# Strided TENSOR_REDUCE for pair minimum and maximum, a list meeting through PSUM, and a reordered pipeline on SyncE, GpSimd, ScalarE and TensorE

## The reference

```python
dist = jnp.sqrt((diff * diff * m_h).sum(axis=-1) + 1e-08)   # to the 64 tokens of the causal window
dist = jnp.where(mask[None], dist, jnp.inf)
neg_d, loc = jax.lax.top_k(-dist, K)                        # K = 32 nearest of 64
infl = jnp.exp(-topd); infl = infl / (infl.sum(-1, keepdims=True) + 1e-08)
context = jnp.einsum('btk,btkd->btd', infl, neighbor_v)
context = context + gate * 0.1 * (q_unit @ (hebb_U[h] @ hebb_V[h]))
outs.append(q_h * context)                                  # then the decoder, the second norm and the experts
```

## Time and profile before

| quantity | value |
|---|---|
| median of three runs | 994.27 us |
| profiled execution, time / span | 990.1 / 988.3 us |
| busy: TensorE, VectorE, ScalarE, GpSimd | 748.7, 771.6, 501.0, 521.6 us |
| mean granted TensorE clock | 0.722 of full speed |
| first and last theta reduction (64 of them) | 98.7 and 958.0 us |

### The profile page before, as it was taken

The page is one execution under the profiler, slowest core; times in us unless marked ns, Lnnn a source line. Parts: engine busy times, 40 slices in busy tenths (PEclk is TensorE's granted clock), DMA queues, the critical chain, the costliest instruction groups (busy, mean ns, idle before and its releaser), DMA issues. The chain is left out here.

```text
span 988.3 us, 21942 instructions
## 1 busy us (share of the span) xinstructions
PE 748.7 (76%) x5686; PEld 534.6 (54%) x5749; DVE 771.6 (78%) x5082; ACT 501.0 (51%) x1542; POOL 521.6 (53%) x811
## 2 busy tenths in 40 slices
PE   5977776777687766678688767789688777788765
PEld 3444554554465545555466546566466554666554
DVE  5857998788778887778787787788887887787861
ACT  3952455554455445544455445554455544555452
POOL 2113475555645565556655565565655656555452
PEclk8985777887857688876766686765766777766665
DMA  5300000000000000000000000000000000000000
GB/s 158 97 3 13 14 10 18 16 17 15 19 18 15 14 19 19 16 15 16 19 18 15 14 19 18 15 17 16 18 19 15 18 14 19 19 16 17 15 14 11
DMA packets 41181, 21.18 MB, mean 21 GB/s; under 512 B 6040, under 2 KB 40544, under 8 KB 41056
## 3 DMA queue, kind: packets, MB, share of 16 engines
q1 hardware_dynamic: 41056, 19.77, 7.0%
HBM read 10.44 MB, written 4.19 MB: 15 GB/s over the span
## 5 line engine op out<-in xcount | busy, mean ns | idle before, releaser
L984 DVE MAX8 gsgn_all<-modn_all 128x8 f32<-128x32 f32 x2048 | 204.2, 172 | 0.0
L740 ACT ACTIVATE nst<-psC 16x192 f32<-16x192 f32 x64 | 20.5, 320 | 287.6 <-PE psC L1276 287.6
L990 DVE MATCH_REPLACE8 modn_all<-gsgn_all,modn_all 128x32 f32<-128x32 f32 x1024 | 166.1, 173 | 0.0
L554 POOL TENSOR_TENSOR big<-big,con 128x512 f32<-128x512 f32 x128 | 162.7, 1293 | 4.8 <-DVE big L1033 4.8
L505 POOL TENSOR_SCALAR n_c<-x,nm_c,rs_c 128x128 f32<-128x128 f32 x64 | 29.4, 460 | 248.4 <-ACT nm_c L678 244.5
L1235 PE MATMUL psC<-vst,big 128*128 128x68 f32 x512 | 120.6, 324 | 43.1 <-ACT n L781 41.5
L1015 DVE SCALAR_TENSOR_TENSOR key<-psD,key 128x512 f32<-128x512 f32 x64 | 44.1, 690 | 126.5 <-ACT key L701 126.3
L1193 PE MATMUL psD<-mask_bf,ident_bf 128*128 128x320 bf16 x256 | 69.9, 419 | 94.3 <-DMA tst<-nst 93.3
L1235 PEld LDWEIGHTS psC<-vst,big 128*128 128x128 f32 x512 | 97.8, 238 | 54.5 <-issue 51.2
L1236 PE MATMUL psC<-vst,big 128*128 128x68 f32 x512 | 120.8, 325 | 0.0
L1236 PEld LDWEIGHTS psC<-vst,big 128*128 128x128 f32 x512 | 99.0, 240 | 0.0
(11 more groups left out here) (208 smaller groups left out, 1795.0 us busy)
## 6 DMA issues: line engine op xcount, KB each, us to landing
tst<-qT_all SPq DMA_DIRECT2D x256, 17.0 KB
big<-in_x SPq DMA_DIRECT2D x16, 256.0 KB, 2.9
xs<-in_x SPq DMA_DIRECT2D x64, 64.0 KB, 1.9
out<-yo SPq DMA_DIRECT2D x64, 64.0 KB, 1.6
sst<-nst SPq DMA_DIRECT2D x128, 3.0 KB
tst<-nst SPq DMA_DIRECT2D x128, 2.0 KB
con<-in_consts SPq DMA_DIRECT2D x1, 581.5 KB, 6.1
wmod_sb<-in_wmod SPq DMA_DIRECT2D x1, 384.0 KB, 4.5
```

What stands on the lines that cost most here:

```text
L554: nc.gpsimd.tensor_tensor(wab[:, k % 2, v].rearrange("p (r t) -> p r t", r=4), wsel.rearrange("p (r t) -> p r t", r=4), part.unsqueeze(1). ...
L984: last = v.max(top[:, u, h, where], low_high[:, u, h])
L990: last = v.match_replace(low_high[:, u, h], top[:, u, h, 0:8], low_high[:, u, h], GONE)
```

## The change

- VectorE: the maximum, the minimum and the negation become two TENSOR_REDUCE instructions over a view whose innermost dimension is the pair, 32 elements apart. `meet` no longer reads two lists from SBUF: the negated high list is written to PSUM (`pHigh`, in bank 1 of `psW`) and `meet` reads it there. Den and reciprocal of chunk i-2 move ahead of `d2` and of `drop(1)`.
- SyncE: the output DMA goes to the end of the step, behind the rows.
- GpSimd: `sqs` and `sst` go ahead of `n_c`.
- PSUM: `pN` and `pNN` move from `psC` into free columns of bank 0 of `psW`.
- TensorE: context products first, then the `diff` transposes, values, `pN` (i+3), `pNN` (now i+2), counting and the rest. The context products no longer wait for `n2`; the key transposes now wait for `nst` of chunk i+3 and `n2` of chunk i+2.
- ScalarE: `lnn`/`rnn` go to the front, `cst` ahead of the Signs, `vst`, `nst` and `n2` (now i+2) behind the Signs, the last Exp to the end of the step.

The PSUM columns:

```diff
+        pHigh = psW[:, 1, 0:2 * NH * 8].rearrange("p (h n) -> p h n", h=NH)
         pC = psC[:, 0:8 * VP]
-        pN = psC[0:2 * NH, 8 * VP:8 * VP + 3 * WIN]
-        pNN = psC[:, 8 * VP + 3 * WIN:8 * VP + 3 * WIN + NH]
+        pN = psW[0:2 * NH, 0, 3 * WIN:6 * WIN]
+        pNN = psW[:, 0, 6 * WIN:6 * WIN + NH]
```

SyncE:

```diff
             def step(i):
-                k = i - 4
-                if there(k):
-                    sync.wait_ge(yo_ready, k + 1)
-                    sync.dma_start(oc[:, k], yo[:, k % 2]).then_inc(out_in[k % 2], 16)
                 k = i + 3
...
                     sync.dma_start(xs[:, k % 4], xc[:, k]).then_inc(xs_in[k % 4], 16)
+                k = i - 4
+                if there(k):
+                    sync.wait_ge(yo_ready, k + 1)
+                    sync.dma_start(oc[:, k], yo[:, k % 2]).then_inc(out_in[k % 2], 16)
```

VectorE, pairs and meeting:

```diff
-                    x4 = key[:, i % 2].rearrange("p (h u j) -> p h u j", h=NH, u=2)
+                    x4 = key[:, i % 2].rearrange("p (h u j) -> p h j u", h=NH, u=2)
                     dve.wait_ge(d2_ready, i + 1)
                     need(dve, theta_ready, i)
-                    v.tensor_tensor(low_high[:, 1], x4[:, :, 0], x4[:, :, 1], ALU.max).then_inc(pair_done, 1)
-                    v.tensor_tensor(low_high[:, 0], x4[:, :, 0], x4[:, :, 1], ALU.min).then_inc(pair_done, 1)
-                    dve.wait_ge(pair_done, 3 * i + 1)
-                    v.tensor_scalar(low_high[:, 1], low_high[:, 1], -1.0, None, ALU.mult).then_inc(pair_done, 1)
-                    dve.wait_ge(pair_done, 3 * i + 2)
+                    v.tensor_reduce(low_high[:, 0], x4, AX_X, ALU.min).then_inc(pair_done, 1)
+                    v.tensor_reduce(low_high[:, 1], x4, AX_X, ALU.max, negate=True).then_inc(pair_done, 1)
+                    dve.wait_ge(pair_done, 2 * i + 1)
...
-                    v.scalar_tensor_tensor(out=meet, in0=top[:, 1], scalar=-1.0, in1=top[:, 0], op0=ALU.mult,
+                    need(dve, w_ready, i)
+                    v.tensor_scalar(pHigh, top[:, 1], -1.0, None, ALU.mult).then_inc(high_done, 1)
+                    dve.wait_ge(high_done, i + 1)
+                    v.scalar_tensor_tensor(out=meet, in0=pHigh, scalar=0.0, in1=top[:, 0], op0=ALU.max,
                                            op1=ALU.max).then_inc(meet_done, 1)
```

TensorE, the products ahead of counting, and the waits ahead of the key transposes:

```diff
+                k = i + 3
+                if there(k):
+                    need(pe, n2_ready, k - 1)
+                    pe.wait_ge(opnd_ready, k + 1)
+                    for g in range(NG):
+                        last = mm(pN, selm[:, k // CPB, g], sqs[:, g], start=(g == 0), stop=(g == NG - 1))
+                    last.then_inc(pn_ready, 1)
+                k = i + 2
+                if there(k):
+                    pe.wait_ge(nst_ready, k + 1)
+                    mm(pNN, nst[:, k % 2, WIN:3 * WIN], con[0:2 * NH, C_ID + NH:C_ID + 2 * NH], start=True,
+                       stop=True).then_inc(pnn_ready, 1)
...
                 k = i + 1
                 if there(k):
                     pe.wait_ge(d2_ready, k + 1)
                     need(pe, vst_ready, 2 * (k - 1))
+                    pe.wait_ge(nst_ready, min(k + 3, NCH))
+                    pe.wait_ge(n2_ready, min(k + 2, NCH))
```

ScalarE, behind the Signs:

```diff
+                need(act, pnn_ready, min(i + 3, NCH))
+                need(act, pn_ready, min(i + 4, NCH))
                 k = i - 1
                 if there(k):
                     act.wait_ge(v_ready, k + 1)
...
+                k = i + 3
+                if there(k):
+                    s = k % 2
+                    need(act, rows_in[s], ROWS_IN * (k // 2))
+                    nc.scalar.activation(nst[:, s], pN, ACT.Copy).then_inc(nst_ready, 1)
```

More of the change, by code:

```diff
@@ L518, in step @@
                                             ALU.mult).then_inc(s_ready, 1)
+                k = i - 4
+                if there(k):
+                    pool.wait_ge(nm_done, k + 1)
+                    pool.wait_ge(rs_done, k + 1)
+                    need(pool, pn2_ready, k - 1)
+                    nc.gpsimd.tensor_scalar(n_c[:, k % 2], x2[:, k % 2], nm_c[:, k % 2:k % 2 + 1], rs_c[:, k % 2:k % 2 + 1],
+                                            ALU.add, ALU.mult).then_inc(nc_ready, 1)
                 k = i + 1
@@ L1009, in step @@
                         expert_matrices(1)
-                k = i + 1
-                if there(k):
-                    dve.wait_ge(outer_ready, k + 1)
-                    e = key[:, k % 2].rearrange("p (h j) -> p h j", h=NH)
-                    v.scalar_tensor_tensor(out=e, in0=pB, scalar=0.0, in1=e, op0=ALU.max, op1=ALU.min).then_inc(d2_ready, 1)
-                if there(i):
-                    dve.wait_ge(picked, 6 * i + 2)
-                    drop(1)
                 k = i - 2
@@ L1026, in step @@
                     v.tensor_scalar(den[:, s], cst[:, s, :, HD], 1e-8, None, ALU.add).then_inc(den_done, 1)
+                k = i + 1
+                if there(k):
+                    dve.wait_ge(outer_ready, k + 1)
+                    e = key[:, k % 2].rearrange("p (h j) -> p h j", h=NH)
+                    v.scalar_tensor_tensor(out=e, in0=pB, scalar=0.0, in1=e, op0=ALU.max, op1=ALU.min).then_inc(d2_ready, 1)
+                k = i - 2
+                if there(k):
+                    dve.wait_ge(den_done, k + 1)
+                    v.reciprocal(rden[:, k % 2], den[:, k % 2]).then_inc(rden_ready, 1)
+                if there(i):
+                    dve.wait_ge(picked, 6 * i + 2)
+                    drop(1)
                 k = i - 1
@@ L1034, in step @@
                                            op1=ALU.mult).then_inc(w_ready, 1)
-                k = i - 2
-                if there(k):
-                    dve.wait_ge(den_done, k + 1)
-                    v.reciprocal(rden[:, k % 2], den[:, k % 2]).then_inc(rden_ready, 1)
                 if there(i):
@@ L1207, in step @@
             def step(i):
+                k = i - 2
+                if there(k):
+                    blk = 2 * (k % CPB)
+                    if k == 0:
+                        pe.wait_ge(gb_ready, 2)
+                    pe.wait_ge(vst_ready, 2 * k + 2)
+                    need(pe, cst_ready, 2 * k)
+                    pe.wait_ge(wab_ready, 2 * k + 2)
+                    for r in range(4):
+                        cols = slice(r * P, (r + 1) * P)
+                        o = pC[:, r * 2 * VP:(r + 1) * 2 * VP].rearrange("p (v x) -> p v x", v=2)
+                        mm(o, wab[:, k % 2, 0, cols], vst[:, blk + 1:blk + 3, r], start=True, stop=False)
+                        last = mm(o, wab[:, k % 2, 1, cols], vst[:, blk:blk + 2, r], start=False, stop=True)
+                    last.then_inc(c_ready, 1)
                 k = i - 1
                 if there(k):
-                    pe.wait_ge(ln_done, min(k + 2, NCH))
+                    pe.wait_ge(diff_ready, k + 1)
+                    need(pe, w_ready, k)
+                    for r in range(4):
+                        last = nc.tensor.transpose(pDT[:, r * P:(r + 1) * P], diff[:, r * P:(r + 1) * P], ident)
+                    last.then_inc(dT_ready, 1)
+                need(pe, ln_done, min(i + 1, NCH))
+                k = i - 1
+                if there(k):
                     for n, blk in enumerate(new_blocks(k)):
@@ L1265, in step @@
                     distances(k % 2).then_inc(dist_ready, 1)
-                k = i + 3
-                if there(k):
-                    pe.wait_ge(opnd_ready, k + 1)
-                    need(pe, cst_ready, 2 * (k - 4))
-                    if k <= 2:
-                        pe.wait_ge(gatew_ready, (3, 4, 4)[k])
-                    if k == 3:
-                        pe.wait_ge(gb_ready, 1)
-                    for g in range(NG):
-                        last = mm(pN, selm[:, k // CPB, g], sqs[:, g], start=(g == 0), stop=(g == NG - 1))
-                    last.then_inc(pn_ready, 1)
                 k = i + 1
@@ L1298, in step @@
                     nc.tensor.transpose(pO, osp[:, k % 2], ident).then_inc(po_ready, 1)
-                k = i + 3
-                if there(k):
-                    pe.wait_ge(nst_ready, k + 1)
-                    mm(pNN, nst[:, k % 2, WIN:3 * WIN], con[0:2 * NH, C_ID + NH:C_ID + 2 * NH], start=True,
-                       stop=True).then_inc(pnn_ready, 1)
             steps(step, routing)
```

112 lines of the change are left out of this document (40 added, 72 removed).

## The result

The changed kernel takes 757.09 us (median of four runs, 753.96 to 763.18) against 995.06 us before. The ratio is 0.762, with a 95% interval of 0.757 to 0.767. The forecast was 882 us with a range of 825 to 945: the direction holds, and so does the ring that it put first; the size does not. The profiled execution took 757.29 us, its span is 755.5 us.

What follows compares the result with a forecast made beforehand. The ring through SyncE's output DMA bounds the kernel at 13.79 us a step. Mixing 10.5 and 13.7 us gives 11.9; 58 steps gain 110 us, five opening steps 2: 878 us profiled, 882 median, range 825 to 945.

Steps and rivals of the forecast that it cites:

- the ring that it put first: Loop from `yo` through SyncE's output DMA, rows, masks and distances, Ln, back to `yo`: 13.79 us a step.
- What bounds the kernel now: The loop through SyncE's output DMA bounds; VectorE comes next, from five opening steps of 11.9 us where no output is issued.
- The output DMA goes last: On SyncE, rows no longer stand behind a late `yo`; the 1.6 us a step of row wait goes.
- Pairs: VectorE's pair reductions: 1080 ns each taken, between 690 and 1230; gain 0.2 us a step.
- Meeting: VectorE's `meet` through PSUM: copy 0.25, `meet` 0.29 and 0.05 us between; gain 0.35 us a step.
- VectorE's step: VectorE's busy time a step falls from 11.07 to 10.5 us, between 9.8 and 11.6.
- TensorE and ScalarE: Their order decides once SyncE is out; half-clock time at 13.7 and full-clock time at 10.5 us mix to 11.9 a step.
- a share of 0.5: Part of step time with TensorE at full clock, up from 0.44 once the 1.6 us row wait goes.
- a clock far from 0.75: Sign of error: a granted TensorE clock far from 0.75 on either side would make the sum wrong.
- Zero prices: Moves put at nothing: GpSimd's `sqs` and `sst` ahead of `n_c`, `d2` behind `cst`, ScalarE late with `nst`.
- VectorE alone: Rival: clock stays high, reductions take 690 ns, VectorE 9.8 us busy; step 10.4 us, 797 us; chance 0.12.
- The slower rival: TensorE held at half clock through the whole main stage: 14.6 us a step, 1040 us; chance 0.07.

Runs made afterwards that it cites:

- e1: The kernel before with only the output DMA moved to the end of SyncE's step: 846.8 us, ratio 0.852.
- e4: The changed kernel with the output DMA put back to the front of SyncE's step: 817.2 us, ratio 0.819.
- e9: The changed kernel with 16 extra 256-element reductions of various strides and pairs after VectorE's last step: 0.6 us each at stride 4 or 8.
- e6: The changed kernel with the old `meet` of two SBUF lists: 776.7 us, ratio 0.784.
- e2: The kernel before with only VectorE's two edits (pair reductions, meeting through PSUM), all orders old: 989.4 us, ratio 0.996.
- e13: The kernel before with six filler matmuls a step in TensorE's wait for the rows: 926.8 us, ratio 0.932.
- e7: The changed kernel with both pair reductions issued twice: 814.9 us, ratio 0.823.
- e12: The changed kernel with `n_c` ahead of `sqs` and `sst` on GpSimd again: 766.4 us, ratio 0.774.
- e3: The kernel before with output DMA last and VectorE's two edits, old orders on TensorE, ScalarE and GpSimd: 826.8 us, ratio 0.831.
- e5: The changed kernel with the old pair code (maximum, minimum, negation): 841.2 us, ratio 0.850.
- e17: The changed kernel with twelve filler matmuls a step before TensorE's wait for `wab` and the last eight MAX8 writing to PSUM: 716.2 us, ratio 0.721.

## Why the prediction was wrong

**What bounds the kernel now: right.** The ring through the output DMA was the bound (e1, e4), and VectorE came next (e1). One reading is slightly off: the opening stage is not wholly without output, its first output DMA is issued at 150.3 us, in the last of the five steps.

**The output DMA goes last: right, and larger than priced.** The row wait was taken at 1.6 us a step; e1 gained 2.5 us a step in the main stage, from 13.79 to 11.32. What a broken ring gives back is not the wait seen on it but the distance to the next bound, and that was VectorE's 11.2 us, at either level of the clock.

**Pairs: the mis-sized term.** 1080 ns were taken, 696 are measured, the 690 of the low end. I scaled the one strided reduction in the trace, but that is a long run at stride 8, and the pair view is two alternating unit streams (e9). The rule of the Trainium skill that a reduction runs at one element a cycle (VectorE: DVE Perf Modes, Rules for kernel authors) gave the right price here, and the line rule (SBUF — State Buffer, Door 1) holds for strides 4 and 8 in e9 but not for this view. By the prediction's own formula the 0.8 us between the two rules would be 30 us of the kernel, and not some 20.

**Meeting: right.** The copy and `meet` take 0.29 us each with 0.04 between; the gain is 0.32 for 0.35, and 20 us in e6.

**VectorE's step: wrong, mostly through the pairs.** 10.5 were forecast; 9.37 busy and a floor of 9.47 are measured. First pair to first pick fell by 1.07 us where 0.2 were forecast, and that is 0.87 of the 1.13 missing. VectorE's two edits alone take 1.6 us off its busy time (e2).

**TensorE and ScalarE: here the sum failed.** The step is "So a step takes 13.7 in half-clock time and 10.5 in full-clock time", mixed by "a share of 0.5". Both the share and the price of half-clock time are wrong.

The share is 0.76 (clock 0.88). I only took the wait away and let the clock stand for the work; but the clock was itself part of the ring (e13): in the old kernel a wait of TensorE cost its own length and then half speed in the work behind it. The prediction had named a clock far from 0.75 as a sign of being wrong.

The price of 13.7 holds for a step at half clock from end to end, as in the earlier trace rows. A step that is only partly at half clock is made good by TensorE's slack in the rest, as long as VectorE's step leaves it that slack. e7 shows it at nearly the forecast VectorE step, 10.6 us busy: with the floor of 10.8 and the full-clock share of 0.38 of its slower step the formula gives 12.4 us, and the step takes 10.84. With a floor of 9.47 the slack is too short, and a step at a clock of 0.69 takes 10.88.

How the 2.0 us between 11.9 and 9.9 divide is an estimate. Had VectorE's step been the forecast 10.5, the excess over it would lie between that of e7 (0.03 at 10.8) and that of e6 (0.39 at a floor of 9.85, mean step 10.24), so a step would take 10.5 to 10.9. Then 1.0 to 1.4 us are the half-clock term, and the other 0.6 to 1.0 VectorE's step, mostly the pairs. Measured floor and measured share put into the formula together still give 10.2, 0.3 too many: the formula itself does not hold. Why the clock rises after some stretches and not after others stays open; that filling waits raises it is shown in both kernels.

**Zero prices.** GpSimd's order was priced at nothing and is worth 9 us: with `n_c` and its wait back ahead of `sqs`, which `pN` needs, TensorE waits 28.5 us for `sqs` (e12). The moves of TensorE and ScalarE had a price for what they may cost and none for what they gain; together with GpSimd's and with den and reciprocal they are the 70 us between e3 and the changed kernel. `d2` behind `cst` cost little, as priced: VectorE waited 10.7 us in all ahead of den.

**Rivals.** "VectorE alone", with 0.12 and 797 us, is what came, with reductions at the low end and a high clock, and even more of it: 9.9 us a step where it had 10.4. The slower rival stood on a clock that stays low when TensorE is dense; it moved the other way. The forecast steps of 11.2 to 12.5 us are 841 to 917 us by the prediction's own sum, and not 846 to 922; this changes nothing.

## What to carry to other kernels

An in-order DMA queue is a ring member: here a store that waits for a late result, issued ahead of loads that feed the next step, paced the whole kernel, and the sign was a long wait on the queue with waits for its loads elsewhere. Where TensorE waits inside such a ring, the wait may be worth more than its length, as the half-clock work behind it was here; a few fillers in the wait show how much. Do not mix two step lengths by the share of time at each clock: a half-clock stretch costs only what the slack of its own step cannot take up, and nothing where another engine's step is long enough. Price each view of an instruction by a row with the same view; a stride in one run of elements and a stride between two streams are different things.

## What the runs showed of the hardware

- Fillers in TensorE's waits paid without any other edit: 68 us of 995 in the old kernel (six a step, clock 0.72 to 0.81), 35 us of 757 in the new one (twelve a step, clock 0.88 to 1.00 in the main stage).
- The same step at a granted clock of 0.69 and of 1.00: 10.84 and 10.81 us where VectorE needs 10.6 (e7), 10.88 and 9.47 where it needs 9.4.
- A reduction of 256 fp32 elements takes 0.41 us at strides 1 and 2 and for pairs 32 elements apart, and 0.6 us at strides 4 and 8.
- MAX8 can write to PSUM at the rate of SBUF: eight in 0.83 us in both places (e17).
- Beside an instruction of GpSimd, a TENSOR_SCALAR of 256 elements from SBUF to SBUF took 865 ns in the mean for 280 (e5), as instructions with two SBUF inputs did. TENSOR_REDUCE from SBUF (682 to 706 ns) and a TENSOR_SCALAR of 128 elements into PSUM (294 to 297 ns) show no such spread in the changed kernel.
